# Groups whose feed-forward runs alone: twelve chunks in twelve neighbouring places instead of every second one

## The chip, the core and the metric

The kernel runs on one core of a Trainium2 chip. The metric is the device time of one execution in microseconds (us), the median of several runs. The engines are named as in the profile: PE (TensorE, matmuls), DVE (VectorE), ACT (ScalarE), POOL (GpSimd) and SP (SyncE, which here only issues DMAs). Each works through its own instruction list in order, and they meet only at semaphores.

## What is computed

A macaron block over 32 sequences of 256 tokens with 128 features, in float32:

```
x = x + 0.5 * ffn(layernorm(x))        # stream f1
x = x + attention(layernorm(x))        # stream at: linear attention, 16 heads of 8, elu+1 features, rope
x = x + 0.5 * ffn(layernorm(x))        # stream f2, same weights as f1

ffn(x): probs = sigmoid(x @ router.T); two best of 8 experts, weights normalised to 1
        h = square(relu(x @ W1e)); out = sum over the two experts of weight * (h @ W2e)
```

The experts are four of width 128 and four of width 256, so 1536 hidden columns in all. The kernel computes all of them for every token and scales each expert's hidden columns by a gate weight, which is zero for experts that were not chosen.

## The kernel before

**Tiling.** The tokens are cut into 16 groups of two sequences (512 tokens). Each group passes through f1, then at, then f2. A feed-forward pass of one group is 12 chunks of 128 hidden columns (NC = 12). Float32 accuracy is had from a split of each operand into a high and a low part, so a product is three matmuls.

**One chunk c of group n in stream s** is this chain:
1. PE `up` (L496 to L498): three matmuls into one of two PSUM banks (c even or odd). It waits until `weighted` of chunk c-2 has freed the bank.
2. DVE `weighted` (L1025, writes `hid`): relu times the root of the gate weight `g_all`. `hid` has six slots, so it waits for `remainders` of chunk c-6.
3. ACT `squares`: the square (L719), then the rounded high part `h_hi` (L730). Within a call for three places the order is square 0, square 1, high 0, square 2, high 1, high 2.
4. POOL `remainders`: the low part `h_lo` (L858).
5. PE `down` (L514 to L516): three matmuls that add into bank `yp[s]`. It stands 9 places behind `up` (DOWN_BEHIND).

After chunk 11 ACT copies the sum (`copy_yT`, L741), PE transposes it (`back`, L533), and DVE adds it to x (`add_moe`, L1033).

**The gate weights of the next group** are made while this one runs: `logits` (PE, L477), `exp_logits` (ACT, L697 and L701), best two and their weights (DVE), `root_of_weights` (POOL, L852), `spread_roots` (DVE, L1003 and L1009), `weight_rows` (PE, L467), `rows_of_weights` (ACT, L709). Then SP writes 32 rows to memory (L382) and reads them back spread over all partitions (`broadcast`, four pieces, L394) into `g_all`, which the first `weighted` of the next group waits for.

**The order is written out by hand.** All engines run the same iterations t = -3 to 21. An iteration has 24 places (PLACES), and the function `chunks(t, place)` tells which chunks stand at a place. In iteration t the f1 stream works on group t+1 from place 0, and the f2 stream on group t-4 from place 12 (SHIFT = 5). Between the places stands the rest: on PE, for instance, the transposes of f1 come before place 0; the attention state of group t-2 (`state`, L589) and the logits of f1 after places 0 to 2; `weight_rows` of f2 after place 5; `back` of f2 and the transpose of f2 after place 11; the output projection, `q` and the logits of f2 after place 14; `weight_rows` of f1 after place 17; `kv` (L547) after place 20; `back` of f1 at the end. On DVE the end of the iteration is `rope_k` and `rope_k_sum` (L1084), and the next one begins with `k_features` (L1089) and `q_features` (L1064), before place 0; ACT's `exp_k` (L751) stands between the two.

**Three kinds of iteration.** In t = 4 to 13 both streams run in full. In t = -1 to 3 only f1 has chunks (groups 0 to 4); f2 has them alone from t = 15, and the groups 10 to 15 of f2 (t = 14 to 19) reach into such iterations. For these eleven groups the function `alone(s, t)` is true: their chunks stand at every second place (step = 2), so that they spread over 24 places, and `back`, `copy_yT`, `add_moe` and `store` of these groups stand half an iteration from where they stand for the others, with the other stream's PSUM bank for the transposes.

## Time and profile before

| | |
|---|---|
| median of 3 runs | 803.7 us (803.64 to 804.73) |
| the profiled execution | 804.86 us |
| its span, first to last instruction | 803.1 us |
| PE / POOL busy | 725.4 us (90%) / 686.8 us (86%) |
| ACT / DVE busy | 598.4 us (75%) / 582.8 us (73%) |
| mean granted TensorE clock | 0.974 |
| POOL busy, 200 to 600 us, of each 100 | 97.2 to 98.8 us |
| POOL busy, 0 to 100, 100 to 200, 600 to 700 us | 69.7, 76.4, 78.0 us |

The view of the span in slices shows POOL and PE busy nine tenths or more in the middle, and less at both ends. A row of the timeline is: start, duration, engine, line, operation, tile written and tiles read, count of merged instructions; in brackets the idle time before it and what ended that. In the chain of work that ended last a row is: start, duration, engine or DMA, tile and line. Durations of matmuls are modelled up to their end in the array, while the next one starts earlier; the distance of two starts is what one costs.

### The profile page before, as it was taken

What the parts mean: (1) busy time and instruction counts of PE and PEld (TensorE: products, weight loads), DVE (VectorE), ACT (ScalarE), POOL (GpSimd) and SP (SyncE); (2) the same over time, 40 slices, a digit from 0 to 9 for tenths busy, and PEclk for the clock granted to TensorE, in tenths of its full rate; (3) what the DMA queues carried; (4) which work ended last, traced back from release to release, by engine and by line L of the source; (5) the groups of instructions that cost most, each with busy time, mean ns of one, the idle gap of its engine ahead of it and who ended that gap; (6) DMA issues with size and microseconds to landing.
All of it is one profiled execution on the core that took longest, in us unless ns stands there. A gap on an engine that the chain in (4) does not pass through costs nothing.

```text
span 803.1 us, 13042 instructions
## 1 busy us (share of the span) xinstructions
PE 725.4 (90%) x3600; PEld 589.8 (73%) x3600; DVE 582.8 (73%) x1832; ACT 598.4 (75%) x1219; POOL 686.8 (86%) x668
## 2 busy tenths in 40 slices
PE   1779888889999999999999999999999987978987
PEld 1557666667788888888888888888887866866755
DVE  3445689787969787877878796978786768577533
ACT  3577677657787978888888888797878776656755
POOL 3778868869999999999999999999999868667865
PEclk9999899989999999999999999999999999899989
DMA  5544022033233221333323233322223311303330
GB/s 177 184 162 130 13 95 106 1 105 107 106 107 119 85 94 49 129 97 106 119 107 120 107 120 105 119 76 101 66 104 107 119 61 46 120 2 118 119 119 26
DMA packets 31159, 79.36 MB, mean 99 GB/s; under 512 B 3312, under 2 KB 14448, under 8 KB 31088
## 3 DMA queue, kind: packets, MB, share of 16 engines
q1 hardware_dynamic: 30800, 78.47, 28.9%
q8 instruction: 29, 0.48, 0.2%
q14 instruction: 42, 0.34, 0.1%
q10 hardware_dynamic: 288, 0.07, 0.1%
HBM read 73.81 MB, written 4.72 MB: 98 GB/s over the span
## 4 chain that ended last, share of the span: by engine, by line
POOL 39%; PE 21%; DVE 18%; issue 9%; ACT 8%; DMA 4%; DVEq 0%; POOLq 0%; SPq 0%; ACTq 0%
POOL h_lo L858 26%; DVE hid L1025 5%; POOL root_f L852 4%; DMA g_all_f<-rows_f 3%; PE bank L496 3%; PE bank L514 3%; POOL rstd_f L837 2%; PE bank L498 2%; PE bank L497 2%; PE bank L516 2%; PE bank L515 2%; ACT h_hi L730 2%; POOL x_lo_f L846 2%; ACT xn_f L676 2%; PE bank L589 2%
## 5 line engine op out<-in xcount | busy, mean ns | idle before, releaser
L858 POOL TENSOR_TENSOR h_lo<-hid,h_hi 128x512 fp32r<-128x512 f32 x384 | 493.5, 1311 | 79.1 <-ACT h_hi L730 78.7
L1025 DVE SCALAR_TENSOR_TENSOR hid<-bank,g_all_f 128x512 f32<-128x512 f32 x384 | 262.5, 685 | 151.3 <-PE bank L498 109.5
L719 ACT ACTIVATE hid<-hid 128x512 f32<-128x512 f32 x384 | 228.8, 622 | 52.0 <-DVE hid L1025 51.5
L730 ACT ACTIVATE h_hi<-hid 128x512 fp32r<-128x512 f32 x384 | 225.6, 620 | 4.9 <-ACT hid L719 0.8
L496 PE MATMUL bank<-x_hi_f,w_hi 128*128 128x512 f32 x384 | 166.8, 434 | 16.4 <-DVE hid L1025 15.8
L514 PE MATMUL bank<-h_hi,w_hi 128*128 128x512 f32 x384 | 156.7, 408 | 17.3 <-ACT yT L741 10.4
L498 PE MATMUL bank<-x_hi_f,w_lo 128*128 128x512 f32 x384 | 154.7, 403 | 0.0
L515 PE MATMUL bank<-h_lo,w_hi 128*128 128x512 f32 x384 | 154.0, 401 | 0.0
L497 PE MATMUL bank<-x_lo_f,w_hi 128*128 128x512 f32 x384 | 153.8, 401 | 0.0
L516 PE MATMUL bank<-h_hi,w_lo 128*128 128x512 f32 x384 | 153.6, 400 | 0.0
L496 PEld LDWEIGHTS bank<-x_hi_f,w_hi 128*128 128x128 f32 x384 | 74.4, 194 | 41.4 <-DVE hid L1025 24.9
L514 PEld LDWEIGHTS bank<-h_hi,w_hi 128*128 128x128 f32 x384 | 74.0, 193 | 39.8 <-POOL h_lo L858 14.0
L498 PEld LDWEIGHTS bank<-x_hi_f,w_lo 128*128 128x128 f32 x384 | 74.0, 193 | 18.2
L516 PEld LDWEIGHTS bank<-h_hi,w_lo 128*128 128x128 f32 x384 | 73.5, 191 | 17.1
L515 PEld LDWEIGHTS bank<-h_lo,w_hi 128*128 128x128 f32 x384 | 73.9, 192 | 16.1
L497 PEld LDWEIGHTS bank<-x_lo_f,w_hi 128*128 128x128 f32 x384 | 74.7, 195 | 11.1
L676 ACT ACTIVATE xn_f<-x_sb,nbias_f,rstd_f 128x128 f32<-128x128 f32 x128 | 52.4, 481 | 7.8 <-POOL nbias_f L839 7.8
L852 POOL TENSOR_TENSOR root_f<-cwt_f,c_half 128x8 f32<-128x8 f32 x32 | 54.6, 1706 | 0.0
L846 POOL TENSOR_TENSOR x_lo_f<-xT,x_hi_f 128x512 fp32r<-128x512 f32 x32 | 41.6, 1299 | 14.0 <-DVE x_hi_f L943 14.0
L688 ACT ACTIVATE xT<-bank 128x512 f32<-128x512 f32 x48 | 28.4, 591 | 29.0 <-PE bank L458 19.1
L943 DVE CAST x_hi_f<-xT 128x512 fp32r<-128x512 f32 x32 | 21.5, 671 | 26.8 <-ACT xT L688 26.8
L697 ACT ACTIVATE ex_f<-bank 128x32 f32<-128x32 f32 x32 | 6.3, 198 | 45.1 <-PE bank L477 45.1
(102 smaller groups left out, 1021.3 us busy)
## 6 DMA issues: line engine op xcount, KB each, us to landing
g_all_f<-rows_f SPq DMA_DIRECT2D x128, 512.0 KB, 5.5
x_sb<-in_x SPq DMA_DIRECT2D x16, 256.0 KB, 3.3
out_x<-x_sb SPq DMA_DIRECT2D x16, 256.0 KB, 7.1
g_all_f<-in_w SPq DMA_DIRECT2D x2, 768.0 KB, 6.8
con<-in_const SPq DMA_DIRECT2D x1, 584.0 KB, 6.4
rows_f<-g_row_f SPq DMA_DIRECT2D x32, 16.0 KB, 1.4
g_all_f<-in_wqkv SPq DMA_DIRECT2D x1, 192.0 KB, 6.5
con<-in_const ACTq DMA_DIRECT2D x1, 68.0 KB, 3.2
```

The source lines that it names most:

```text
L496: mm(o, w1_hi[:, w], x_hi[s][u][:], start=True, stop=False)
L497: mm(o, w1_hi[:, w], x_lo[s][u][:], start=False, stop=False)
L498: mm(o, w1_lo[:, w], x_hi[s][u][:], start=False, stop=True).then_inc(s_p1[s], 1)
L514: mm(o, w2_hi[:, c, :], h_hi[:, c, :], start=(c == 0), stop=False)
L515: mm(o, w2_hi[:, c, :], h_lo[:, c, :], start=False, stop=False)
L516: i = mm(o, w2_lo[:, c, :], h_hi[:, c, :], start=False, stop=(c == NC - 1))
L676: i = fn(xn[s][:, k, :], tile, ACT.Identity, bias=nbias[s][:, k:k + 1], scale=rstd[s][:, k:k + 1])
L719: fn(h, h, ACT.Square).then_inc(s_sq[s], 1)
L730: fn(h_hi[:, c, :], hid[:, c % STAGE, :], ACT.Copy).then_inc(s_hhi[s], 1)
L852: gp.tensor_tensor(root[s][:], cwt[s][:], c_half[:], ALU.pow).then_inc(s_root[s], 1)
L858: gp.tensor_tensor(h_lo[:, c, :], hid[:, c % STAGE, :], h_hi[:, c, :].bitcast(F32), ALU.subtract).then_inc(s_hlo[s], 1)
L1025: v.scalar_tensor_tensor(hid[:, c % STAGE, :], hp[c % 2][:], 0.0, g_all[s][:, EXPERT[c], :], ALU.max, ALU.mult).then_inc(s_z[s], 1)
```

## The change

The function `alone` is removed, with every branch on it. All groups have their chunks at neighbouring places: f1 at places 0 to 11 of iteration n-1, f2 at places 12 to 23 of iteration n+4. `down` stays 9 places behind, so in an iteration of f1 alone places 12 to 20 hold only `down`, and 21 to 23 nothing. `back`, `copy_yT`, `add_moe` and `store` of all groups stand where they stood for the groups of full iterations: `copy_yT` of f1 after place 17, `back` of f1 at the end of the iteration and `add_moe` after place 2 of the next; for f2, `copy_yT` after place 5, `back` after place 11, and `add_moe` after place 14. The transposes go into the stream's own bank. No instruction on data is added or removed; only order and waits differ.

```diff
--- before.py
+++ after.py
@@ -326,11 +326,6 @@
 
             return done(t + 1 + (1 if s == "f2" else 0) - off[other[s]])
 
-        def alone(s, t):
-
-
-            return not live(t + 1 - SHIFT) if s == "f1" else not live(t + 2)
-
         def chunks(t, place, behind=0):
 
 
@@ -338,10 +333,9 @@
             for s, start in (("f1", 0), ("f2", NC)):
                 for back in range(2):
                     k = place + PLACES * back - start - behind
-                    step = 2 if alone(s, t - back) else 1
                     n = t - back + 1 - off[s]
-                    if live(n) and k % step == 0 and 0 <= k // step < NC:
-                        out.append((s, n, k // step, back))
+                    if live(n) and 0 <= k < NC:
+                        out.append((s, n, k, back))
             return out
 
         x_dram = x_in.rearrange("b (p r) d -> p b (r d)", r=RT)
@@ -410,10 +404,7 @@
                     load_pairs(4, 3)
                 if first_time(True, t + 1):
                     load_pairs(10, NG // 2 - 5)
-                if alone("f2", t - 2):
-                    store(t - 1 - SHIFT)
-                if not alone("f2", t - 1):
-                    store(t - SHIFT)
+                store(t - SHIFT)
 
             first_part = WHERE["expert"][1]
             load(0, 0)
@@ -502,10 +493,7 @@
                 pe.wait_ge(s_hlo[s], value(n * NC + c + 1))
                 if c == 0:
                     if due(n):
-                        if alone(s, t0 - 1):
-                            pe.wait_ge(s_yT[s], value(n))
-                        else:
-                            pe.wait_ge(s_x[s], value(n))
+                        pe.wait_ge(s_x[s], value(n))
                     if s == "f2" and not due(n):
                         pe.wait_ge(s_x["f1"], SHIFT)
                     if first_time(s == "f1", n):
@@ -523,12 +511,6 @@
                     return
                 pe.wait_ge(s_yT[s], value(n + 1))
                 o = yp[s]
-                if alone(s, t0):
-                    o = yp[other[s]]
-                    if due(n):
-                        pe.wait_ge(s_x[s], value(n))
-                    if s == "f2":
-                        pe.wait_ge(s_x["f1"], NG)
                 for k in range(TG):
                     i = nc.tensor.transpose(o[:, k * D:(k + 1) * D], yT[:, k * P:(k + 1) * P], ident)
                 i.then_inc(s_y[s], 1)
@@ -634,10 +616,7 @@
                 transpose("at", t - 1, t, 2)
                 quarter(t, 3, par)
                 attn_transpose(t - 2)
-                if alone("f1", t - 1):
-                    back("f1", t, t - 1)
-                if not alone("f2", t - 1):
-                    back("f2", t - SHIFT, t - 1)
+                back("f2", t - SHIFT, t - 1)
                 transpose("f2", t + 2 - SHIFT, t, 3)
                 quarter(t, 4, par)
                 out_proj(t - 2)
@@ -649,10 +628,7 @@
                 kv(t - 1, 0)
                 kv(t - 1, 1)
                 quarter(t, 7, par)
-                if alone("f2", t - 1):
-                    back("f2", t - SHIFT, t - 1)
-                if not alone("f1", t):
-                    back("f1", t + 1, t)
+                back("f1", t + 1, t)
 
             pipeline(pe, iteration)
 
@@ -780,11 +756,8 @@
                 rows_of_weights("f2", n2)
                 if not live(t - SHIFT):
                     norm("f1", t + 3)
-                if alone("f1", t - 1):
-                    copy_yT("f1", t, t - 1)
                 evacuate_x("at", t - 1, t, 1)
-                if not alone("f2", t - 1):
-                    copy_yT("f2", n2_last, t)
+                copy_yT("f2", n2_last, t)
                 squares(t, 2)
                 squares(t, 3)
                 copy_attnT(t - 2)
@@ -801,10 +774,7 @@
                 if first_time(True, t + 2):
                     act.wait_ge(s_w2, 16)
                     fn(w2_hi[:], w2_raw.rearrange("p (c d) -> p c d", c=NC), ACT.Copy).then_inc(s_w2hi, 1)
-                if not alone("f1", t):
-                    copy_yT("f1", n1, t)
-                if alone("f2", t - 1):
-                    copy_yT("f2", n2_last, t)
+                copy_yT("f1", n1, t)
                 squares(t, 6)
                 exp_q(t - 1)
                 copy_v(t - 1)
@@ -1027,7 +997,7 @@
 
             def add_moe(s, n, t0):
                 if live(n):
-                    y = yp[other[s] if alone(s, t0) else s]
+                    y = yp[s]
                     dve.wait_ge(s_y[s], value(n + 1))
                     tiles = x_sb[:, bass.ds(value(n * TG), TG), :]
                     v.tensor_tensor(tiles, y[:].rearrange("p (k d) -> p k d", k=TG), tiles, ALU.add) \
@@ -1132,8 +1102,6 @@
                 n1, n2, n2_last = t + 2, t + 2 - SHIFT, t + 1 - SHIFT
                 if first_time(True, t + 1):
                     split_attention_weights()
-                if alone("f2", t - 2):
-                    add_moe("f2", t - 1 - SHIFT, t - 2)
                 k_features(t - 2)
                 q_features(t - 2)
                 weighted(t, 0)
@@ -1142,8 +1110,7 @@
                 weighted(t, 1)
                 spread_roots("f2", n2_last, 1)
                 weighted(t, 2)
-                if not alone("f1", t - 1):
-                    add_moe("f1", t, t - 1)
+                add_moe("f1", t, t - 1)
                 weighted(t, 3)
                 stats("f1", t + 3, (par + 1) % 2)
                 weighted(t, 4)
@@ -1174,10 +1141,7 @@
                 weighted(t, 13)
                 spread_roots("f1", n1, 1)
                 weighted(t, 14)
-                if alone("f1", t - 1):
-                    add_moe("f1", t, t - 1)
-                if not alone("f2", t - 1):
-                    add_moe("f2", t - SHIFT, t - 1)
+                add_moe("f2", t - SHIFT, t - 1)
                 weighted(t, 15)
                 rope_q_sin(t - 1)
                 weighted(t, 16)
```

## Rows read from the trace of the kernel before

**Rows 1.** The page: the chain that ended last, by engine.
```profile
POOL 39%; PE 21%; DVE 18%; issue 9%; ACT 8%; DMA 4%; DVEq 0%; POOLq 0%; SPq 0%; ACTq 0%
```

**Rows 2.** The page, groups of POOL: busy and mean ns, idle before.
```profile
L858 POOL TENSOR_TENSOR h_lo<-hid,h_hi 128x512 fp32r<-128x512 f32 x384 | 493.5, 1311 | 79.1 <-ACT h_hi L730 78.7
...
L852 POOL TENSOR_TENSOR root_f<-cwt_f,c_half 128x8 f32<-128x8 f32 x32 | 54.6, 1706 | 0.0
L846 POOL TENSOR_TENSOR x_lo_f<-xT,x_hi_f 128x512 fp32r<-128x512 f32 x32 | 41.6, 1299 | 14.0 <-DVE x_hi_f L943 14.0
```

**Rows 3.** Busy time by stage (length, then PE, PEld, DVE, ACT, POOL, clock): full iterations.
```profile
400.00:500.00 100.00, 99.43 (x516) 82.64 (x515) 79.41 (x255) 84.26 (x175) 98.53 (x95) 1.00 0.33 111
```

**Rows 4.** Timeline of POOL: the first h_lo of f1 groups 0 to 5.
```profile
29.64 1.29 POOL L858 TENSOR_TENSOR h_lo<-hid,h_hi 128x512 fp32r<-128x512 f32 x1 [0.50 <-ACT h_hi L730]
...
32.56 2.53 POOL L858 TENSOR_TENSOR h_lo<-hid,h_hi 128x512 fp32r<-128x512 f32 x2
...
53.89 1.30 POOL L858 TENSOR_TENSOR h_lo<-hid,h_hi 128x512 fp32r<-128x512 f32 x1 [0.49 <-ACT h_hi L730]
...
78.77 1.30 POOL L858 TENSOR_TENSOR h_lo<-hid,h_hi 128x512 fp32r<-128x512 f32 x1 [0.48 <-ACT h_hi L730]
...
108.99 1.27 POOL L858 TENSOR_TENSOR h_lo<-hid,h_hi 128x512 fp32r<-128x512 f32 x1 [0.98 <-ACT h_hi L730]
...
139.30 1.27 POOL L858 TENSOR_TENSOR h_lo<-hid,h_hi 128x512 fp32r<-128x512 f32 x1 [1.34 <-ACT h_hi L730]
...
178.08 2.54 POOL L858 TENSOR_TENSOR h_lo<-hid,h_hi 128x512 fp32r<-128x512 f32 x2 [4.54 <-ACT h_hi L730]
```

**Rows 5.** Timeline of PE, ACT and DVE around the first handover.
```profile
28.61 0.63 PE L496 MATMUL bank<-x_hi_f,w_hi 128*128 128x512 f32 x1
...
43.78 0.34 ACT L709 ACTIVATE g_row_f<-bank,c_cut 32x128 f32<-32x128 f32 x1
...
47.67 0.40 PE L496 MATMUL bank<-x_hi_f,w_hi 128*128 128x512 f32 x1
...
48.37 1.03 PE L477 MATMUL bank<-router_sb,xT 128*128 128x96 f32 x8
...
51.00 0.69 DVE L1025 SCALAR_TENSOR_TENSOR hid<-bank,g_all_f 128x512 f32<-128x512 f32 x1 [4.95 <-DMA g_all_f<-rows_f]
```

**Rows 6.** The chain that ended last, at the handover of f1 group 3 to 4.
```profile
131.77 0.70 DVE ka L1084
...
135.01 1.13 PE bank L589 x8
136.15 0.88 PE bank L477 x8
```

**Rows 7.** Timeline of POOL: h_lo of f2 groups 10 to 15.
```profile
635.73 2.56 POOL L858 TENSOR_TENSOR h_lo<-hid,h_hi 128x512 fp32r<-128x512 f32 x2 [0.59 <-ACT h_hi L730]
...
668.07 2.54 POOL L858 TENSOR_TENSOR h_lo<-hid,h_hi 128x512 fp32r<-128x512 f32 x2 [0.95 <-ACT h_hi L730]
...
700.74 3.80 POOL L858 TENSOR_TENSOR h_lo<-hid,h_hi 128x512 fp32r<-128x512 f32 x3 [0.95 <-ACT h_hi L730]
...
731.55 3.79 POOL L858 TENSOR_TENSOR h_lo<-hid,h_hi 128x512 fp32r<-128x512 f32 x3 [1.86 <-ACT h_hi L730]
...
754.96 3.79 POOL L858 TENSOR_TENSOR h_lo<-hid,h_hi 128x512 fp32r<-128x512 f32 x3 [0.49 <-ACT h_hi L730]
...
777.97 3.76 POOL L858 TENSOR_TENSOR h_lo<-hid,h_hi 128x512 fp32r<-128x512 f32 x3 [4.71 <-ACT h_hi L730]
...
793.57 3.77 POOL L858 TENSOR_TENSOR h_lo<-hid,h_hi 128x512 fp32r<-128x512 f32 x3 [0.37 <-ACT h_hi L730]
```

**Rows 8.** The chain that ended last, at the handover of f2 group 11 to 12.
```profile
695.99 0.89 PE bank L620 x8
696.88 0.70 PE bank L547 x3
697.58 0.87 PE bank L477 x8
```

**Rows 9.** The core's span and its mean granted TensorE clock.
```profile
core 0: 803.1 us, clock 0.974
```

## The prediction

> **What bounds the kernel now.** The page comes first: the chain that ended last runs through POOL for 39% of the span, more than through any other engine [rows 1]. The busy time by stage then splits the kernel: in the full iterations POOL is busy 98.5 us of 100 and PE 99.4 [rows 3], so nothing that leaves POOL's work alone can change them. The change leaves that work alone everywhere: the same 384 h_lo and their neighbours. All that it can move is the time in which POOL has nothing to do, and the page gives that as 79.1 us before h_lo, nearly all for ACT's h_hi [rows 2]. It lies at the two ends, where one stream runs alone.
>
> So I read POOL's timeline there, by the start of each group's first h_lo (called T0 below). For f1 the distances are 24.25, 24.88, 30.22, 30.31 and 38.78 us [rows 4]; for f2 groups 10 to 15 they are 32.34, 32.67, 30.81, 23.41 and 23.01 us, and the last group takes 19.37 us to 797.34 [rows 7]. POOL's own work in such a distance is less: 12 h_lo back to back, by 1.265 us (2.53 for two), are 15.2; one inverse deviation is 1.67 (what lies between the first and second h_lo rows [rows 4], less the first one's 1.29, is 1.63, with 0.04 of handover); a root is 1.71 and a low part of x is 1.30 [rows 2]. An iteration of f1 with attention holds 15.2 + 2 x 1.67 + 1.71 + 2 x 1.30 = 22.8 us of work and takes 30.2. These iterations are therefore bound by a loop of waits from group to group, not by an engine. The chain shows which: rope sum, k features, attention state, logits, and only then the squares of the new group [rows 6]; in the first two iterations it is the fetch of the gate weights [rows 5].
>
> **What the change does to that loop.** With neighbouring places a group is a burst that POOL can take at its own pace, and then nothing of the group is left to lie beside the serial work between two groups. I cost each handover as burst + gap and compare with today's distance. Two things lengthen the gap. First, places 0 to 2 now hold three `up` instead of two, and the third waits for the first `weighted`; `state` and `logits` stand behind it on PE, and `exp_logits` stands ahead of the first square on ACT. Second, what waits on the `down` of late chunks (`weight_rows` behind chunk 8, `kv` behind chunk 11) now waits for POOL to be nearly through the group; today, at every second place, the same instructions stand behind the `down` of chunks 4 and 5 (places 17 and 19, less 9, halved).
>
> *Start of group 0.* Today the logits (48.37 in the next iteration) are done before the first `weighted` at 51.00, and h_lo follows 2.89 us behind it [rows 4, 5]. Afterwards: weighted 0.7, third `up` 0.7 (three matmuls, 47.67 to 48.37), logits 1.03, exp and add about 0.6 with their handovers, then two squares and one high part, about 1.8 (2.89 less the 0.69 of `weighted` and 0.4 of handovers). That is 4.9 us, 2.0 more, and 0.4 more again because TensorE is at half clock just there (0.63 us for a matmul that takes 0.40 later [rows 5]): **+2.4**.
>
> *Handovers 0 to 1 and 1 to 2 (no attention yet), bound by the gate weights.* From T0: nine h_lo, one inverse deviation, the root: 9 x 1.265 + 1.67 + 1.71 = 14.8; `down` of chunk 8, 0.7; transpose of the weights, 0.4. The 0.4 is an estimate. From ACT's copy of the rows to `weighted` it is 7.2 us (43.78 to 51.00 [rows 5]), and 4.9 from there. Sum 28.0, against 24.25 and 24.88: **+3.7 and +3.1**. Bounds: 27 if the exp hides, 29.5 if the burst has the idle 1.3 us that a half of a full iteration shows (1.47 of 100 us idle [rows 3], rounded up for the loss of the other stream as cover).
>
> *Handovers 2 to 3 and 3 to 4, bound by attention.* Burst 15.2 + 1.67 + 1.71 + 1.30 = 19.9. Gap: `down` of chunk 11, 0.75; `kv`, 12 matmuls of half the columns, 1.4 by the 0.70 for three full ones, and 0.3 until the last is out; the last rope pair 0.75 (an estimate, little more than one pass of DVE over the tile, 0.70 [rows 6]). From the rope sum to `state` it is 3.24 us today, and from there to h_lo 4.29 (131.77, 135.01, 139.30 [rows 4, 6]). Between them come the first `weighted` and the third `up`, 1.4. Gap 12.1, distance 32.0 to 33.3; I take 32.6 against 30.22 and 30.31: **+2.3 each**.
>
> *Handover 4 to 5.* Today 38.78, with the first f2 group's statistics and routing between. That work (some 3 us on DVE, the f2 low part 1.30 and root 1.71 on POOL) stays, but for the low part it lies behind the burst in either case. I take 38.0, from 36 to 39.5: **-0.8**.
>
> *Tail, f2 groups 10 to 15.* The transposes, their copies and the first two `up` follow the last `down` within some 4 us and are covered by the gate weights: `weight_rows` stands behind `down` of chunk 8, so ACT's copy of the rows comes 2.2 before the end of the burst at the latest (behind two normalisations), and `weighted` 7.2 later, 5.0 after the burst. Then `weighted` 0.7, the third `up` 0.8, and from the output projection to h_lo 4.75 as today (695.99 to 700.74 [rows 7, 8]): 11.3. Burst 15.2 + 2 x 1.67 + 1.71 = 20.2. Twice 31.5 to 33, taken as 32.3, against 32.34 and 32.67: **0 and -0.4**. With attention running out (one normalisation less, no q, one inverse deviation less): 18.6 + 9.9 = 28.5 to 29.5, taken as 29.0, against 30.81, **-1.8**. Without attention (no output projection, 0.9): 18.6 + 9.1 = 27.7 against 23.41, **+4.3**; then 16.9 + 7.1 = 24.0 against 23.01 (no logits any more; the gate weights are last), **+1.0**. The last group has nothing beside it and runs at POOL's pace, 15.7 against 19.37: **-3.7**. What follows its last h_lo is the same.
>
> `back`, `copy_yT`, `add_moe` and the stores are costed at nothing: f1's `copy_yT` and `back` lie beside `kv` and rope (in the first two iterations beside the fetch), f2's `back` is within the 4 us above. A store now waits on SP for `add_moe` at place 14; the next `broadcast` behind it on that queue is due at places 4 to 6 of the next iteration, so it waits for nothing. If that cover were gone, a late store would delay the gate weights of five tail groups by a microsecond or two each.
>
> **Sum.** Head 2.4 + 3.7 + 3.1 + 2.3 + 2.3 - 0.8 = +13.0; tail -0.6; together **+12.4 us**, of which I take 12. The profiled execution took 804.86 (span 803.1 and 1.8 around it), 1.2 above the median of the runs; 803.7 + 12 = 815.7, stated as 815.5.
>
> **The rivals.**
> *Clock.* TensorE was at half clock for 2 x (1 - 0.974) x 803.1 = 42 us [rows 9], in stretches at the ends, after PE had stood or run thinly. With bursts PE does only one `down` per h_lo in the late part of a group (0.7 us in 1.27) and stands in the gap, so more handovers may meet a half-clock stretch. There the third `up` (0.7 to 1.4, by the two levels) and `state` are on the path, some 1.2 us a handover. If six of the eleven handovers that go undisturbed now are hit, it is +7: **822.5**. Against it: several of today's handovers pay it already. The Trainium skill ("TensorE: Matmul & The Clock Gate", Part 1) says that the array is throttled when it is idle and released by sustained activity, which is this rival's mechanism; the 0.63 and 0.40 us of the same matmul agree with its two levels of 1.2 and 2.4 GHz.
>
> *The other side: faster.* The loop of waits is cut. Today each spread group in the tail stops POOL several times for h_hi, since chunks stand behind rope, state and `kv` in the queues; a burst passes these once. If the gap in attention handovers were 9 us (k features and the third `up` overlapping more than I think) and in the others 6, four distances would be 29 (-2.4 in the head, -6.9 in the tail), the next two 27.6 and 24.6 (-3.2, +1.2), handover 4 to 5 would be 36 (-2.8), the first two of the head and the fifth of the tail as today, the last group -3.7 and the start +1: -16.8, 787, and with half of that **795**. It decides from gaps that are 1.2 us shorter than mine on the mean of the ten handovers (12.4 / 10); from there on the change is a gain. For it: the last group's 3.7 us are sure. Against: every term of the gap has a row, and in the first two handovers 7.2 us of fetch cannot shrink.
>
> *No net change.* Tail gains of 4 to 5 us (all bursts without idle time, no loss at the fourth handover) against a head loss of the same size: **804**.
>
> *The change does less than it says*: order is only a right of way. If up to now chunks were issued as fast as their inputs came anyway, times stay as they are. The stops of POOL for h_hi inside groups speak against it.
>
> **How the numbers follow.** Forecast 0.63, between 808 and 820; clock rival 0.20, 820 to 828; no net change 0.07; faster 0.10. A measurement of this kernel tells about 0.2% (1.6 us) from no change. So slower 0.84, same 0.06, faster 0.10. The range goes from 805 (forecast with the low ends of its gaps, 1 us each at ten handovers) to 827.
>
> **What the profile afterwards would show.** Of POOL, bursts of twelve h_lo without idle time (20 us with attention) and idle stretches of 9 to 12 us between groups. Distances of first h_lo of 28, 28, 32.6, 32.6 and 38 in the head, and 32, 32, 29, 28, 24 and a last group of 16 in the tail; the middle unchanged. The logits of f1 behind the first `weighted` in t = -1 to 3. More idle time before h_lo, 91 us instead of 79. It would be wrong if the fourth tail handover stays at 23 us, if `kv` isn't the instruction that waits behind `down` of chunk 11, or if the attention handovers come out under 30.

## The result

The changed kernel takes 814.92 us (median of 4 runs, 814.02 to 815.27) against 803.67 us before (802.94 to 804.73): 1.0137 times as long, 95% interval 1.0120 to 1.0155. The profiled execution took 814.99 us with a span of 813.2 us, 10.1 us more than before.

The page after, first the chain that ended last by engine, then the groups that answer to [rows 1, 2]:

```profile
PE 24%; DVE 24%; POOL 24%; issue 12%; ACT 10%; DMA 5%; DVEq 0%; POOLq 0%; ACTq 0%; SPq 0%
...
L828 POOL TENSOR_TENSOR h_lo<-hid,h_hi 128x512 fp32r<-128x512 f32 x384 | 491.3, 1309 | 50.9 <-ACT h_hi L706 50.3
...
L816 POOL TENSOR_TENSOR x_lo_f<-xT,x_hi_f 128x512 fp32r<-128x512 f32 x32 | 41.4, 1293 | 43.7 <-DVE x_hi_f L913 43.7
```

The work of POOL is the same (687.2 us busy, 686.8 before). Its share of the last chain fell from 39% to 24%: more of the chain now runs through DVE (24% instead of 18%), PE (24% instead of 21%) and the time in which no wait shows (issue, 12% instead of 9%). The idle time moved as well. Before h_lo it is 50.9 us instead of 79.1, before the low part of x 43.7 instead of 14.0, because POOL now stands still between two groups, where that instruction is the next one. POOL's whole idle time is span less busy, 813.2 - 687.2 = 126.0 us against 803.1 - 686.8 = 116.3; the difference of 9.7 is nearly the whole loss.

The timeline of POOL after shows how. The rows answer to [rows 4]; of each group of f1 the row of its first h_lo stands here, and for group 3 all its h_lo:

```profile
32.69 2.55 POOL L828 TENSOR_TENSOR h_lo<-hid,h_hi 128x512 fp32r<-128x512 f32 x2 [3.95 <-ACT h_hi L706]
...
59.59 2.53 POOL L828 TENSOR_TENSOR h_lo<-hid,h_hi 128x512 fp32r<-128x512 f32 x2 [2.47 <-ACT h_hi L706]
...
86.30 2.55 POOL L828 TENSOR_TENSOR h_lo<-hid,h_hi 128x512 fp32r<-128x512 f32 x2 [2.48 <-ACT h_hi L706]
...
119.86 2.52 POOL L828 TENSOR_TENSOR h_lo<-hid,h_hi 128x512 fp32r<-128x512 f32 x2 [4.67 <-ACT h_hi L706]
...
124.00 6.30 POOL L828 TENSOR_TENSOR h_lo<-hid,h_hi 128x512 fp32r<-128x512 f32 x5
...
132.04 1.28 POOL L828 TENSOR_TENSOR h_lo<-hid,h_hi 128x512 fp32r<-128x512 f32 x1
...
134.50 5.04 POOL L828 TENSOR_TENSOR h_lo<-hid,h_hi 128x512 fp32r<-128x512 f32 x4
...
151.40 2.50 POOL L828 TENSOR_TENSOR h_lo<-hid,h_hi 128x512 fp32r<-128x512 f32 x2 [3.37 <-ACT h_hi L706]
...
188.91 2.52 POOL L828 TENSOR_TENSOR h_lo<-hid,h_hi 128x512 fp32r<-128x512 f32 x2 [5.60 <-ACT h_hi L706]
```

Group 3 is one burst from 119.86 to 139.54 with no idle time in it, and then POOL has no h_lo for 11.9 us. The tail, answering to [rows 7]:

```profile
645.54 5.08 POOL L828 TENSOR_TENSOR h_lo<-hid,h_hi 128x512 fp32r<-128x512 f32 x4 [1.27 <-ACT h_hi L706]
...
678.77 1.29 POOL L828 TENSOR_TENSOR h_lo<-hid,h_hi 128x512 fp32r<-128x512 f32 x1 [4.05 <-ACT h_hi L706]
...
712.47 2.52 POOL L828 TENSOR_TENSOR h_lo<-hid,h_hi 128x512 fp32r<-128x512 f32 x2 [4.07 <-ACT h_hi L706]
...
742.45 2.55 POOL L828 TENSOR_TENSOR h_lo<-hid,h_hi 128x512 fp32r<-128x512 f32 x2 [3.37 <-ACT h_hi L706]
...
769.26 1.29 POOL L828 TENSOR_TENSOR h_lo<-hid,h_hi 128x512 fp32r<-128x512 f32 x1 [2.48 <-ACT h_hi L706]
...
792.39 15.07 POOL L828 TENSOR_TENSOR h_lo<-hid,h_hi 128x512 fp32r<-128x512 f32 x12 [6.54 <-ACT h_hi L706]
```

The last row is twelve h_lo in one piece, 15.07 us, where the spread group took 19.37. Distances of first h_lo, in us:

| | before | forecast | after |
|---|---|---|---|
| start of group 0 | 29.64 | 32.0 | 32.69 |
| f1 0 to 1 | 24.25 | 28.0 | 26.90 |
| f1 1 to 2 | 24.88 | 28.0 | 26.71 |
| f1 2 to 3 | 30.22 | 32.6 | 33.56 |
| f1 3 to 4 | 30.31 | 32.6 | 31.54 |
| f1 4 to 5 | 38.78 | 38.0 | 37.51 |
| f1 5 to f2 10 (full iterations) | 457.65 | the same | 456.63 |
| f2 10 to 11 | 32.34 | 32.3 | 33.23 |
| f2 11 to 12 | 32.67 | 32.3 | 33.70 |
| f2 12 to 13 | 30.81 | 29.0 | 29.98 |
| f2 13 to 14 | 23.41 | 27.7 | 26.81 |
| f2 14 to 15 | 23.01 | 24.0 | 23.13 |
| the last group | 19.37 | 15.7 | 15.07 |

The rows add to +10.8 us up to group 5, -1.0 in the middle and +0.3 in the tail. They are from one trace of each kernel. kv_early, described below, is the changed kernel but for one move that leaves its time as it is, and its trace has +7.8, -1.0 and +2.5. So the split between head and tail is known to some 3 us only. The chain that ended last, at handover 0 to 1 after, is the forecast's sequence link for link: the eighth and ninth h_lo, `down` of chunk 8 (L502 to L504), the transpose of the weights, ACT's copy, the two transfers, `weighted`, the third `up` (L487 to L489), the logits (L468), exp, squares, high part:

```profile
44.76 2.48 POOL h_lo L828 x2
...
47.28 0.50 PE bank L502
...
48.23 0.12 PE bank L458
...
48.38 0.37 ACT g_row_f L685
...
49.12 1.41 DMA rows_f<-g_row_f
...
50.67 4.03 DMA g_all_f<-rows_f
...
54.73 0.70 DVE hid L995
...
55.47 0.50 PE bank L487
...
56.44 0.88 PE bank L468 x8
...
57.94 0.57 ACT hid L695 x2
...
58.89 0.62 ACT h_hi L706
...
59.59 2.53 POOL h_lo L828 x2
```

From `weighted` at 54.73 to h_lo at 59.59 are 4.86 us, where it was 2.89 [rows 4, 5].

### The profile page after: what moved, and what is told of

The parts are those of the page before. It is cut to its first block, busy times and chain, and to the rows that moved or that the text cites. A ratio compares the mean times of both kernels' runs of the same rounds, so it can differ in the third digit from the quotient of the medians.

```text
span 813.2 us, 12992 instructions
## 1 busy us (share of the span) xinstructions
PE 731.7 (90%) x3600; PEld 582.2 (72%) x3600; DVE 579.8 (71%) x1832; ACT 590.1 (73%) x1219; POOL 687.2 (85%) x668
## 3 DMA queue, kind: packets, MB, share of 16 engines
q1 hardware_dynamic: 30800, 78.47, 27.7%
## 4 chain that ended last, share of the span: by engine, by line
PE 24%; DVE 24%; POOL 24%; issue 12%; ACT 10%; DMA 5%; DVEq 0%; POOLq 0%; ACTq 0%; SPq 0%
POOL h_lo L828 16%; DVE hid L995 6%; POOL root_f L822 4%; DMA g_all_f<-rows_f 3%; PE bank L487 3%; PE bank L468 3%; PE bank L502 3%; PE bank L489 3%; PE bank L488 3%; PE bank L503 2%; PE bank L504 2%; ACT h_hi L706 2%; ACT hid L695 2%; POOL x_lo_at L816 2%; PE bank L571 2%
## 5 line engine op out<-in xcount | busy, mean ns | idle before, releaser
L828 POOL TENSOR_TENSOR h_lo<-hid,h_hi 128x512 fp32r<-128x512 f32 x384 | 491.3, 1309 | 50.9 <-ACT h_hi L706 50.3
L695 ACT ACTIVATE hid<-hid 128x512 f32<-128x512 f32 x384 | 225.7, 620 | 6.2 <-DVE hid L995 5.9
L487 PE MATMUL bank<-x_hi_f,w_hi 128*128 128x512 f32 x384 | 170.4, 444 | 30.4 <-DVE hid L995 29.5
L502 PE MATMUL bank<-h_hi,w_hi 128*128 128x512 f32 x384 | 155.0, 404 | 10.0 <-POOL h_lo L828 9.9
L489 PE MATMUL bank<-x_hi_f,w_lo 128*128 128x512 f32 x384 | 153.8, 401 | 0.0
L503 PE MATMUL bank<-h_lo,w_hi 128*128 128x512 f32 x384 | 152.1, 396 | 0.0
L504 PE MATMUL bank<-h_hi,w_lo 128*128 128x512 f32 x384 | 151.9, 396 | 0.0
L487 PEld LDWEIGHTS bank<-x_hi_f,w_hi 128*128 128x128 f32 x384 | 73.9, 192 | 71.6 <-DVE hid L995 59.9
L502 PEld LDWEIGHTS bank<-h_hi,w_hi 128*128 128x128 f32 x384 | 72.5, 189 | 35.7 <-POOL h_lo L828 20.2
L489 PEld LDWEIGHTS bank<-x_hi_f,w_lo 128*128 128x128 f32 x384 | 73.6, 192 | 17.9
L504 PEld LDWEIGHTS bank<-h_hi,w_lo 128*128 128x128 f32 x384 | 72.4, 189 | 16.6
L816 POOL TENSOR_TENSOR x_lo_f<-xT,x_hi_f 128x512 fp32r<-128x512 f32 x32 | 41.4, 1293 | 43.7 <-DVE x_hi_f L913 43.7
L717 ACT ACTIVATE yT<-bank 128x512 f32<-128x512 f32 x32 | 19.1, 596 | 41.9 <-PE bank L504 41.9
```

The costliest lines, as they stand in the source:

```text
L487: mm(o, w1_hi[:, w], x_hi[s][u][:], start=True, stop=False)
L489: mm(o, w1_lo[:, w], x_hi[s][u][:], start=False, stop=True).then_inc(s_p1[s], 1)
L502: mm(o, w2_hi[:, c, :], h_hi[:, c, :], start=(c == 0), stop=False)
L503: mm(o, w2_hi[:, c, :], h_lo[:, c, :], start=False, stop=False)
L504: i = mm(o, w2_lo[:, c, :], h_hi[:, c, :], start=False, stop=(c == NC - 1))
L695: fn(h, h, ACT.Square).then_inc(s_sq[s], 1)
```

## The experiments

Each has its own runs of the kernel before beside it (median 803.0 to 803.5 us). Where a median and a profiled span differ in a comparison, the text says which it uses.

### Each end alone

```diff
-            return not live(t + 1 - SHIFT) if s == "f1" else not live(t + 2)
+            return False if s == "f1" else not live(t + 2)
```

> The kernel before, with neighbouring places for the five f1 groups only; the f2 groups keep every second place. Theory A (each handover costs its own burst + gap, and the two ends are independent): the head of the changed kernel, +10.9 us over the first handovers (group 5 of f1 starts at 188.9 instead of 178.1), and the tail of the kernel before: 813.5 to 814.5. Theory B (the loss is mainly in the tail, or comes from the two ends together): under 811. Theory C (half clock carries the loss): the time follows the mean granted clock, so 813.5 only if the clock falls under 0.974.

Measured: 812.43 us against 803.46, ratio 1.0113 (1.0097 to 1.0130). Group 5 of f1 starts at 187.5 us, and the clock was 0.982, above that of before. Theory A holds in the place of the loss, the sum is 1 us under its range. Theory C falls: the loss comes with more clock, not less. The profiled execution (810.12) is the fastest of the four. Its head is 9.5 us longer than before, not 10.9, and its tail, spread as before, is about 2.5 us shorter than in the trace of before.

The other end alone, with `not live(t + 1 - SHIFT) if s == "f1" else False`:

> The kernel before, with neighbouring places for the six lone f2 groups only; f1 keeps every second place. Theory A: the distances of the changed kernel's tail, which sum to +0.3 us against the kernel before (+0.9, +1.0, -0.8, +3.4, +0.1, -4.3), and up to 1 us from the entry: 803.5 to 805. Theory B: over 807.

Measured: 808.93 us, ratio 1.0063 (1.0045 to 1.0081). Theory A's 803.5 to 805 is missed, and the number is in theory B's range: by the medians about half as much is lost in the tail as the whole change costs. Its profiled execution, with 812.0 the slowest of the four, has f2 12 to 13 at 31.7 instead of 30.0 in the changed kernel (with a half-clock stretch at 723 to 727 us), f2 13 to 14 at 27.5 instead of 26.8, and its head, which the edit doesn't touch, was 2.0 us later than before. From the first h_lo of f2 group 10 to the end it takes 3.1 us more than before, from that of f1 group 15 4.8 us more. So the tail costs something too, some 3 to 5 us; the +0.3 of the changed kernel's one profiled execution was its good end. The two parts, +9.0 and +5.5, add to 14.5 us where the whole is +11.3. With intervals of 1.3 to 1.5 us on each that is more than they explain; what makes up the rest I can't say.

### Only the places, without the moves

```diff
-                    step = 2 if alone(s, t - back) else 1
+                    step = 1
```

> The kernel before with step = 1 for all groups, but back, copy_yT, add_moe and the stores of the lone groups left in the places and the bank that they had. It separates the places of the chunks from the moves. Theory A (the moves cost nothing): 813.5 to 816, as the changed kernel with 814.9. Rival D (part of the loss is from the moves, since copy_yT of f1 now stands behind the last down at the end of the iteration): 811 or less.

Measured: 820.63 us, ratio 1.0218 (1.0200 to 1.0237). Both theories fall: the moves of `back`, `copy_yT` and `add_moe` are worth 5.7 us to the changed kernel (6.5 by the two ratios), as a gain. One place where they tell is group 1. Timeline of ACT and of PE in this kernel, in group 1:

```profile
62.73 1.64 ACT L676 ACTIVATE xn_f<-x_sb,nbias_f,rstd_f 128x128 f32<-128x128 f32 x4
64.27 0.58 ACT L741 ACTIVATE yT<-bank 128x512 f32<-128x512 f32 x1
```

```profile
64.99 0.47 PE L514 MATMUL bank<-h_hi,w_hi 128*128 128x512 f32 x1 [2.23 <-POOL h_lo L858]
...
70.10 0.60 PE L533 MATMUL bank<-con,yT 128*128 128x128 f32 x4
```

The copy of group 0's sum stands in the next iteration, behind a normalisation of 1.64 us, and the first `down` of group 1 may not write the bank before it. h_lo 0 has been there since 59.5; PE begins `down` at 64.99, stands 2.23 us before it and then works on without a pause, in part at half clock (66 to 69 us). The chain that ended last reaches `weight_rows` at 74.88 through PE alone, while h_lo of chunk 8 had ended at 72.7 and would have let it go some 1.5 us sooner. The bracket names POOL, but h_lo had long been done; the wait ends 0.14 us behind the copy. In the changed kernel the copy lies at the end of its own iteration, in the gap. This handover is 28.68 us long instead of 26.71 in the changed kernel, and a part of the 2 us is the half clock. The two spans differ by 5.6 us: 2.5 up to group 5 (this handover in it), 1.7 in the middle and 1.5 in the tail. What makes up the rest wasn't traced.

### The third up ahead of the logits

The changed kernel, with PE's order in lone iterations turned (and the same for the output projection, q and the logits of f2, around place 14):

```diff
-                quarter(t, 0, par)
+                early = 2 if not live(t - SHIFT) else CQ
+                quarter(t, 0, par, 0, early)
                 state(t - 2)
                 logits("f1", t + 2)
+                quarter(t, 0, par, early, CQ - early)
```

> The changed kernel, but in iterations where one stream runs alone PE does the work that stands behind places 0 to 2 (f1: state and logits) or 12 to 14 (f2: output projection, q, logits) after two of the three up, ahead of the third, which waits for the first weighted. Theory A (the third up is on the loop, 1.4 to 2 us a handover): head -2.0 at the start and twice more, -1.4 three times; tail -2 three or four times; in all 13 to 18 us less, 797 to 802. Theory E (the gap is set by the fetch of the gate weights and by attention alone, and the logits hide behind them): 813 to 815.

Measured: 804.51 us (10 runs), ratio to before 1.0017 (1.0003 to 1.0030): 10.4 us less than the changed kernel. Timeline of POOL, the first h_lo of group 5:

```profile
178.46 2.54 POOL L832 TENSOR_TENSOR h_lo<-hid,h_hi 128x512 fp32r<-128x512 f32 x2 [3.82 <-ACT h_hi L710]
```

188.91 in the changed kernel, 178.08 before: between the two traces the head has lost 10.4 us, for which the expectation had 10.2. No work was taken away for that; only one `up` of 0.7 us changed sides with what waited behind it. But the agreement is in part luck. From the first `weighted` to the first h_lo, group 0 takes 6.33 us in the changed kernel, with PE at half clock there, 4.89 in kv_early, with the same order at full clock, and 2.89 here: the order gives the expected 2.0, the clock 1.4 more. Against kv_early the head is 7.4 us shorter, the middle 1.3 longer and the tail 3.1 shorter. The median is 2.5 us above the upper end of theory A's 797 to 802.

In the tail the trace is only 0.9 us shorter than the changed kernel's (from the first h_lo of f1 group 15 to the end 188.4 instead of 189.3), for which 6 to 8 were expected. The third `up` is on the tail's path in the changed kernel. The chain that ended last there, at f2 group 12, whose first h_lo comes at 712.47:

```profile
706.02 0.70 DVE hid L995
...
706.76 0.50 PE bank L487
...
707.73 0.89 PE bank L602 x8
...
709.32 0.88 PE bank L468 x8
```

In this kernel the third `up` stands behind the logits. Timeline of DVE and of POOL, the first `weighted` and the first h_lo of the same group:

```profile
696.92 0.69 DVE L999 SCALAR_TENSOR_TENSOR hid<-bank,g_all_f 128x512 f32<-128x512 f32 x1 [3.30 <-DMA g_all_f<-rows_f]
```

```profile
700.92 1.28 POOL L832 TENSOR_TENSOR h_lo<-hid,h_hi 128x512 fp32r<-128x512 f32 x1 [1.61 <-ACT h_hi L710]
```

That is 4.00 us where it was 6.45; at groups 11, 13 and 14 it is 5.31, 3.98 and 3.71 where it was 6.44, 5.75 and 4.86, 6.5 us less in all. But the distances from group to group shrank much less, because another chain, nearly as long, now ends last: it goes through the attention state, the late `down`, the transposes and the first two `up`. So theory E's number is nearer in the tail, though not its reason.

### exp_logits behind the squares

```diff
-                exp_logits("f1", t + 2)
+                if live(t - SHIFT):
+                    exp_logits("f1", t + 2)
                 squares(t, 0)
+                if not live(t - SHIFT):
+                    exp_logits("f1", t + 2)
```

and in the same way for f2 around `squares(t, 4)`.

> The changed kernel with one move on ACT: where one stream runs alone, exp_logits stands behind the squares of the next three places and not ahead of them. PE's order is that of the changed kernel. Theory A2 (the first squares are held by exp_logits, which waits for logits on PE, behind the first weighted and the third up): first h_lo 2.9 us behind the first weighted at every handover; head -2 at the start and at the next two, -3 at three with attention; tail -3 to -3.6 three times and -2 once: 788 to 794. Rival H (the routing of the next group becomes late by the same amount, so that the gate weights hold the next handover): 800 to 806.

Measured: 806.98 us (10 runs), ratio 1.0040 (1.0023 to 1.0058). The gaps shrank as theory A2 said: from the end of a group's last h_lo to the first of the next 9.7 and 9.5 us instead of 13.9 and 11.9 in the head, 10.1 instead of 12.8 and 13.0 in the tail. But most of it came back inside the bursts: up to group 5 the five gaps are 15.4 us shorter in all, and the five bursts 9.8 us longer. Timeline of POOL, group 0:

```profile
28.92 1.27 POOL L834 TENSOR_TENSOR h_lo<-hid,h_hi 128x512 fp32r<-128x512 f32 x1 [0.50 <-ACT h_hi L706]
30.49 1.28 POOL L834 TENSOR_TENSOR h_lo<-hid,h_hi 128x512 fp32r<-128x512 f32 x1 [0.29 <-ACT h_hi L706]
34.09 0.20 POOL L810 TENSOR_TENSOR ve_f<-mv_f,c_eps 128x4 f32<-128x4 f32 x1 [2.32 <-DVE mv_f L911]
...
35.75 5.07 POOL L834 TENSOR_TENSOR h_lo<-hid,h_hi 128x512 fp32r<-128x512 f32 x4
```

After two h_lo POOL waits 2.32 us for DVE's variance, which stands behind the sigmoid and `weighted`, and those behind PE's logits and fourth `up`, all of which run at half clock here (0.63 us for a matmul of 512 columns). Group 0's burst is 20.9 us here and 18.3 in the changed kernel. So rival H is nearer, 1 us beyond its range, though through this group's own statistics and not through the gate weights: the logits have to be paid for, ahead of the burst or in it.

Both edits in one kernel, exp_late on both streams and the early logits in the head only:

> As the kernel with exp_logits late, and in the f1-alone iterations PE does state and logits after two of the three up, as in the run with early logits; the tail's PE order is that of the changed kernel. Theory A2: squares wait for nothing of the logits in either, so within 2 us of the run with exp_logits late (788 to 794). Rival H: better than that run by 3 us or more, since the logits of the head come 2 us earlier.

Measured: 803.54 us (10 runs), ratio 1.0009 (0.9989 to 1.0028), 3.4 us better than exp_late alone, as rival H said; against logits_early it is 1.0 us.

### Is it kv behind chunk 11?

```diff
-                quarter(t, 6, par)
+                if live(t + 1 - SHIFT):
+                    quarter(t, 6, par)
                 kv(t - 1, 0)
                 kv(t - 1, 1)
+                if not live(t + 1 - SHIFT):
+                    quarter(t, 6, par)
```

> The changed kernel, but while f1 runs alone (t = -1 to 3) PE does kv before the down of chunks 9 to 11 and not behind them. Theory A as forecast (kv waits behind the down of chunk 11 and starts the rope chain): the three handovers with attention shorter by 2 to 3 us each, 806 to 809. Rival F (read from the changed kernel's trace at 135.6 to 143.0 us: DVE works without a stop from the rope of q, which waits for the low part of x on POOL, to the rope sum, so kv comes in time): shorter by 0.3 us at an undisturbed handover and 1 to 2 at one at half clock, 812 to 815.

Measured: 814.59 us, the changed kernel's time. Rival F holds. Timeline of PE and of DVE at handover 3 to 4 in this kernel:

```profile
135.97 0.39 PE L529 MATMUL bank<-wkv_hi,x_hi_at 128*128 128x256 f32 x1 [1.29 <-DVE x_sb L1101]
```

```profile
132.53 1.39 DVE L1017 TENSOR_TENSOR qb<-bank,con 64x512 f32<-64x512 f32 x2 [1.94 <-PE bank L529]
...
139.88 0.69 DVE L1057 SCALAR_TENSOR_TENSOR ka<-ka,kb 128x512 f32<-128x512 f32 x1
```

kv now starts at 135.97, ahead of the last three `down`, and it changes nothing: DVE goes from the rope of q at 132.53 to the rope sum at 139.88 without a pause, 7.35 us. In the changed kernel the same stretch runs from 135.60 to 142.96, 7.36 us, with kv at 140.41. By these rows what bounded the handover was the start of that stretch, q.

So the next kernel moves q, on top of early logits. Its edits, cut to the branch for f1-alone iterations, on PE, POOL and DVE:

```diff
+                if not live(t + 1 - SHIFT):
+                    q(t - 1)
                 out_proj(t - 2)
...
                 remainders(t, 2, 3, 4, 5)
+                if not live(t + 1 - SHIFT):
+                    low_part("at", t - 1, 0)
                 remainders(t, 6)
...
                 weighted(t, 7)
+                if not live(t + 1 - SHIFT):
+                    high_part("at", t - 1, 0)
```

> The kernel with early logits, and in the f1-alone iterations the attention's x is prepared sooner: DVE's high part behind weighted of place 7 (not 10), POOL's low part behind h_lo 5 (not 7), and PE does q ahead of the output projection. kv stays behind the down of chunk 11. Theory F (the handover with attention was bound by DVE's unbroken work from q to the rope sum; with q 3 us sooner kv behind chunk 11 becomes the bound): 0.3 to 1 us less per handover, three times: 801.5 to 803.5 against 804.5. Rival A (kv behind chunk 11 was the bound all along): no change, 804.5.

Measured: 805.26 us (12 runs, 802.12 to 809.40), ratio 1.0028 (1.0011 to 1.0044). With the edit of kv_early as well:

> As attention_early, and kv stands ahead of the down of chunks 9 to 11 in the f1-alone iterations. Theory F (both gates have to be moved together): 2 to 3 us less per handover with attention than with early logits alone, 796 to 799. Rival I (other work of the second half of the iteration, the statistics and the adding of x, holds DVE as long): within 1 us of attention_early.

Measured: 806.02 us (12 runs), ratio 1.0033 (1.0021 to 1.0045). No gain in either, so theory F's numbers fall; those of the rivals A and I hold, but the chain bears out neither of their mechanisms. In the trace of attention_early the two handovers with attention are longer than in that of logits_early, 31.1 and 32.8 us instead of 30.1 and 32.0, so that q was what bounded them is read from the rows and not shown by a gain. The chain that ended last, at handover 2 to 3 of the second kernel, has left the attention:

```profile
99.71 1.44 PE bank L529 x12
...
103.00 0.25 PE bank L504
...
103.28 0.60 ACT yT L727
...
103.93 0.66 PE bank L515 x4
...
107.03 1.13 PE bank L571 x8
```

POOL had finished this group's h_lo at 99.7; the last `down` ends at 103.25, 3.5 us behind. Two things add up there. PE works from 90.10 on without a pause, the first 3.4 us at half clock, and `kv` (the first row) stands ahead of the last three `down`. The traces separate them: the last `down` of this group ends 1.0 us behind the last h_lo in logits_early, 2.0 in attention_early, which has the same half-clock stretch, and at the handover after it 3.3 in kv_early, which has none. Then come the copy, `back`, the transposes and two `up`, and only then `state` at 107.03. With the attention earlier, the end of the feed-forward group is the bound, at nearly the same time. I didn't try to move `back` and the transpose away from there.

### The last group alone

```diff
-                    step = 2 if alone(s, t - back) else 1
                     n = t - back + 1 - off[s]
+                    step = 2 if alone(s, t - back) and not (s == "f2" and n == NG - 1) else 1
```

> The kernel before, with neighbouring places for the last group of f2 alone. Theory A (the last group has no handover behind it, only the burst counts): 4.3 us less, the last h_lo 15.1 us after the first instead of 19.4: 799 to 800.5. Rival G (the last group's 19.4 us in the kernel before were a half-clock stretch at 775 to 782 us and not its places; the spread group had 17.2 without it in another run): 2 us less, 801 to 802.5.

Measured: 801.81 us (12 runs) against 802.99, ratio 0.9978 (0.9960 to 0.9995). Rival G holds: the gain is 1.2 us and not 4.3. Its first three h_lo are late (timeline of POOL):

```profile
778.49 3.82 POOL L858 TENSOR_TENSOR h_lo<-hid,h_hi 128x512 fp32r<-128x512 f32 x3 [4.04 <-ACT h_hi L730]
783.39 11.33 POOL L858 TENSOR_TENSOR h_lo<-hid,h_hi 128x512 fp32r<-128x512 f32 x9 [1.08 <-ACT h_hi L730]
```

16.2 us for the group, with a half-clock stretch at 778 to 781 us. The spread group took 19.4 in the profiled execution of before, but 17.2 in that of f1_compact, where no half-clock stretch met it: 2 of the 4.3 us were the clock's. This is the one kernel measured here that is faster than the kernel before beyond its interval, by little more than the 0.2% that a measurement can tell.

And this tail with the head of attention_kv_early:

> The f1 groups at neighbouring places with logits, attention and kv early, as in attention_kv_early; the f2 groups 10 to 14 at every second place and the last group at neighbouring ones, as in last_group_compact. Theory A (the two ends are independent): group 5 of f1 starts as in attention_kv_early, and the tail takes what it takes in last_group_compact: 795 to 799. If the ends are not independent, over 801.8.

Measured: 803.00 us (12 runs, 800.2 to 804.9), ratio 0.9993 (0.9979 to 1.0008). Its tail is that of last_group_compact (the profiled one took 185 us from the first h_lo of f1 group 15 to the end, against 187), its head starts group 5 at 178.9, where the same edits gave 182.4 in the trace of attention_kv_early. Theory A's 795 to 799 is missed and the number is in the other range, over 801.8; but A had counted on the gain of attention_kv_early, which didn't come, so this says nothing against two independent ends. It beats nothing: the head at neighbouring places, with all that was mended in it, is as good as the spread head and not better.

## Why the prediction was right, point by point

The forecast was +12 us and 815.5; measured were +11.3 and 814.9. The mechanism in the head, burst + gap with the third `up` ahead of the logits, is shown: by the table of distances, by f1_compact, which brings +9.0 us alone, and by logits_early, which takes it away. That the sum comes so near is in part luck. In the two profiled executions the head is 2.2 us under the forecast's +13.0, the middle 1.0 under its nothing and the tail 0.9 over its -0.6; and by f2_compact the tail costs 3 to 5 us, for which the forecast had a small gain.

- **Start of group 0**, +2.4: +3.1 here. The 4.9 us from `weighted` to h_lo measured 4.86 at the next handover and 4.89 here in kv_early, so the term itself was right. What was too small is the 0.4 for the half clock: the same stretch took 6.33 us in the changed kernel, 1.4 more, because the third `up` and the logits ran at half clock in full. In the kernel before, the logits were done ahead of that stretch. The forecast had read the half clock from durations, 0.63 and 0.40 us; the distance of two starts, which is what a matmul costs, is 0.43 and 0.23.
- **Gate-weight handovers**, 28.0: 26.90 and 26.71, 1.2 too high. The part from ACT's copy to `weighted` was 6.35 us (48.38 to 54.73), not 7.2: the read-back landed in 4.03 us instead of 4.92.
- **Attention handovers**, 32.6 each: 33.56 and 31.54, right on the mean. But the step that named kv behind chunk 11 was wrong. kv does wait there (140.41), but kv_early shows that it doesn't bind; DVE's 7.36 us from q to the rope sum ended at the same time, by chance. The sum was right because the two chains are equally long. The 2 us between the two handovers goes with the half clock: in the changed kernel's trace only the first has such stretches (101 to 105 and 115 to 118 us), and f1_compact repeats both, 33.55 with two stretches and 31.53 with none.
- **Handover 4 to 5**, 38.0: 37.51.
- **Tail**, -0.6: +0.3 in the profiled execution, and 3 to 5 by f2_compact. The gaps with attention were 12.8 and 13.0 instead of 12.1 of the working with its allowance. The term that was short is the start of the fetch: ACT's copy of the gate weights was to come 2.2 us before the burst ends, and at the second of these handovers it begins at 699.83, 0.4 behind the last h_lo, since the two normalisations ahead of it take until then. Most terms had the right sign: f2 13 to 14 longer by 3.4 (forecast 4.3), the last group shorter by 4.3 (3.7). But f2 11 to 12 came out 1.0 longer (forecast 0.4 shorter). Of the last group's 4.3, last_group_compact gives 1.2 to the places, the rest is the clock and what stood around it. The third `up` is on the tail's path, as forecast; what the forecast didn't have is a second chain that is nearly as long, so taking it off gained 0.9 us against the changed kernel's trace and 3.1 against kv_early's.
- **back, copy_yT and add_moe at nothing**: right for the sum, since they lie in the gap, but for a reason that I didn't see. Left where they were they would cost 5.7 us, of which the handover shown above accounts for 2.
- **The clock rival**, 822.5: wrong in its number, and the granted clock moved the other way. Before, TensorE ran at half clock for 42 us; after, the mean granted clock is higher:

```profile
core 0: 813.2 us, clock 0.986
```

That is 2 x (1 - 0.986) x 813.2 = 23 us. All four runs of the changed kernel show 0.986 to 0.990, those of the kernel before 0.970 to 0.982. The difference is smaller than it looks, since not all half clock is counted. For 21 to 32.8 us the changed kernel's profile says that the full clock was granted (first row; length, busy time of PE, PEld, DVE, ACT and POOL, clock), but its matmuls took the 0.63 us of the half clock until then and 0.40 from there:

```profile
21.00:32.80 11.80, 9.04 (x27) 7.04 (x26) 3.33 (x8) 3.68 (x8) 4.83 (x3) 1.00 0.64 225
```

```profile
30.69 0.63 PE L488 MATMUL bank<-x_lo_f,w_hi 128*128 128x512 f32 x1
...
33.06 0.40 PE L488 MATMUL bank<-x_lo_f,w_hi 128*128 128x512 f32 x1
```

Before, the same shows from 21.6 to 24.5 us only. So half clock reached some 45 us before and 34 after, and just there it cost the changed kernel 1.4 us on the path. That denser work is the cause of the rest is not shown. The Trainium skill ("TensorE: Matmul & The Clock Gate", Part 1) says that activity releases the throttle, and the changed kernel's trace agrees in direction; but step_only has its chunks at neighbouring places too, and its runs show 0.978 to 0.985.
- **More idle time before h_lo, 91 us**: wrong, it is 50.9. The idle time went to the instruction that comes first after the gap, the low part of x. The total rose by 9.7.

## What to carry to other kernels

When one stream runs alone and a loop of waits leads from group to group, putting its pieces close together makes each piece of work denser and leaves the serial links between groups bare; spreading them lets the links run beside the work. Cost such a change as burst + gap for each handover, and look for any instruction of the next group that stands, in some engine's list, ahead of the first piece and waits for it indirectly. Here one extra `up` ahead of the logits was worth ten microseconds, seven or more of them in the six handovers of the head. Moving a wait that only seemed to be last (kv) was worth nothing, because another chain ended at the same time; and in the tail, taking the `up` off the path brought little for the same reason. The chain that ends last tells what to shorten, not how much that pays.

## What the hardware did that I had not expected

The half-clock time by the granted clock fell from 42 to 23 us although the kernel became slower, and the granted clock left out a stretch of 11 us at the start in which matmuls ran at half clock. In the kernels with the attention early the half clock also did harm after its stretch: with 3.4 us of it at 90 to 94 us, PE ended the group's `down` 2.0 us behind POOL in attention_early, at 101.81, where it is 1.0 us without such a stretch. And the same transfer, the read-back of the gate weights, took 4.03 us in one chain and 4.92 in another at the same handover, which alone moves that handover by nearly a microsecond.
